# A graph layer on one Trainium2 core: x enters the gate products in three f32r products, x plus beta moves within its turn, and setup and passage are re-ordered

## The reference

```python
h = concat([x[src], x[dst]])
msgs = silu(h @ W1.T + b1) @ W2.T + b2
agg = segment_sum(msgs, src) / (count(src) + 1e-08)
gi, gh = agg @ w_ih.T + b_ih, x @ w_hh.T + b_hh
r, z = sigmoid(i_r + h_r), sigmoid(i_z + h_z)
n = tanh(i_n + r * h_n)
x_new = (1 - z) * n + z * x
y = layernorm(x + gamma * layernorm(x_new) + beta)
```

## Time and profile before

| | |
|---|---|
| median of 3 runs | 2478.14 us (2478.11 to 2478.32) |
| profiled execution, its time | 2478.47 us |
| its span | 2476.8 us, mean granted clock of TensorE 0.987 |
| busy | PE 2301.0, PEld 1622.0, DVE 2122.0, ACT 1496.2, POOL 1332.4 us |
| DMA | 520.31 MB, mean 210 GB/s |

### The profile page before, as it was taken

One profiled execution on the slowest core, in us unless ns is written; L12 is line 12 of the kernel. 1 busy time (PEld: TensorE's weight loads), 2 busy tenths in 40 slices (PEclk: granted clock), 3 DMA queues, 4 the chain that ended last, 5 costly groups with the idle time before them and its releaser, 6 DMA issues.

```text
span 2476.8 us, 46628 instructions
## 1 busy us (share of the span) xinstructions
PE 2301.0 (93%) x10234; PEld 1622.0 (65%) x10234; DVE 2122.0 (86%) x6136; ACT 1496.2 (60%) x2955; POOL 1332.4 (54%) x1475
## 2 busy tenths in 40 slices
PE   4999999999999995999999999999999999999995
PEld 2888888888888883655555555555555555555553
DVE  4777777777777764899999999999999999999998
ACT  2444444444444442577767777777677777777776
POOL 3444444444444421566666666666666666666663
PEclk9999999999999997999999999999999999999998
DMA  3566666666666655666666666666666666666662
GB/s 105 213 232 227 229 230 228 230 227 231 225 233 225 234 209 193 200 216 216 213 210 213 214 217 205 216 207 210 203 212 213 210 205 212 215 209 212 209 204 94
DMA packets 192600, 520.31 MB, mean 210 GB/s; under 512 B 51362, under 2 KB 53946, under 8 KB 192572
## 3 DMA queue, kind: packets, MB, share of 16 engines
q1 hardware_dynamic: 117308, 313.53, 36.2%
q0 software_dynamic: 75264, 206.47, 25.5%
HBM read 468.02 MB, written 206.73 MB: 272 GB/s over the span
## 4 chain that ended last, share of the span: by engine, by line
DVE 42%; PE 37%; issue 15%; DVEq 3%; DMA 1%; ACT 1%; SPq 0%; POOL 0%; POOLq 0%; ACTq 0%
PE banks L893 34%; DVE zd L824 6%; DVE xn L830 5%; DVE st L871 5%; DVE diff L819 5%; DVE rhn L807 5%; DVE tg L835 4%; DVE uu L846 4%; PE banks L905 4%; DVE oh L798 3%; DVE ag L877 2%; DVE ve L860 1%; DVEq L798 1%; DVEq L191 1%; DVE nm L855 1%
## 5 line engine op out<-in xcount | busy, mean ns | idle before, releaser
L893 PE MATMUL banks<-whh,xts 128*128 128x512 f32 (+1 forms) x3136 | 1089.9, 485 | 0.0
L893 PEld LDWEIGHTS banks<-whh,xts 128*128 128x128 f32 x3136 | 552.4, 190 | 312.5 <-issue 281.7
L346 POOL DMA_INDIRECT mg<-messages,rows_now x392 | 408.1, 1041 | 170.4 <-POOL rows_now L383 87.1
L404 POOL TENSOR_TENSOR xb<-xs,betab 128x512 f32<-128x512 f32 x196 | 249.0, 1270 | 372.5 <-ACT rz L501 372.5
L346 POOL DMA_INDIRECT xsrc<-in_x,src_now x196 | 187.3, 956 | 438.5 <-PE banks L905 433.0
L893 PE MATMUL banks<-mg,oh 128*128 128x512 f32 (+1 forms) x1568 | 322.1, 348 | 108.7 <-issue 57.2
L893 PEld LDWEIGHTS banks<-mg,oh 128*128 128x128 f32 x1568 | 253.2, 189 | 214.9 <-issue 158.7
L525 ACT ACTIVATE yy<-uu,nmr,rs 128x256 f32<-128x256 f32 x392 | 214.0, 593 | 293.0 <-DVE nmr L866 293.0
L513 ACT ACTIVATE banks<-banks,rcount 128x768 f32<-128x768 f32 x392 | 326.7, 871 | 38.0 <-PE banks L893 24.9
L471 ACT ACTIVATE msg<-banks 128x512 fp32r<-128x512 f32 (+1 forms) x392 | 192.8, 492 | 246.7 <-PE banks L893 218.3
L625 DVE TENSOR_TENSOR msg<-banks,msg 128x512 fp32r<-128x512 f32 (+1 forms) x392 | 199.9, 552 | 160.1 <-issue 137.7
(11 more groups left out here) (129 smaller groups left out, 4248.8 us busy)
## 6 DMA issues: line engine op xcount, KB each, us to landing
messages<-msg SPq DMA_DIRECT2D x196, 772.0 KB
xts<-in_xt SPq DMA_DIRECT2D x196, 256.0 KB
xs<-in_x SPq DMA_DIRECT2D x196, 256.0 KB
out_y<-yy SPq DMA_DIRECT2D x196, 256.0 KB, 5.1
mg<-messages,rows_now POOLq DMA_INDIRECT x392
xsrc<-in_x,src_now POOLq DMA_INDIRECT x196
xdst<-in_x,dst_now POOLq DMA_INDIRECT x196
oh<-counts SPq DMA_DIRECT2D x196, 2.0 KB
```

Of the source, the lines that this page charges most:

```text
L346: nc.gpsimd.indirect_dma_start(out=dst_tile, out_offset=None, in_=rows, in_offset=bass.IndirectOffsetOnAxis(ap=table, axis=0), bounds_chec ...
L404: nc.gpsimd.tensor_tensor(out=xb[:, u, :], in0=xs[:, u, :], in1=betab[:, :], op=ALU.add)\
L893: return nc.tensor.matmul(out_, lhsT, rhs, start=start, stop=stop, skip_group_check=skip)
```

## The change

x enters the gate products as its f32r high part times both parts of `whh` plus its low part times the high one. `xh` is made by ScalarE at the end of its turn, `xl` by GpSimd behind `tg`. `add_beta` moves to the end of GpSimd's turn and waits for `ag` (aggregate1) instead of the gates. The one hots move behind `st` with lag 2. The transposed load is issued one turn earlier. In the setup the order of the weight loads changes, the row vectors of the biases are loaded as broadcasts, their TensorE products go, and the chain of bias steps runs beside the first edge slots. In the passage the table, the counts, the fill of `mg` (now ScalarE and GpSimd) and the count stores run beside the last edge slots, and a sigmoid over one column is run ahead of the node stage. Some tiles change their place in memory.

```diff
-        whh = sb("whh", [P, KC, G3])
+        wxh, wxl = sb("wxh", [P, KC, G3], f32r), sb("wxl", [P, KC, G3], f32r)
...
+        xh, xl = sb("xh", [P, QU, 2 * D], f32r), sb("xl", [P, QU, 2 * D], f32r)
...
-        def edge_slots(eng, part, first=0):
+        def edge_slots(eng, part, first=0, also=None):
             for n in range(first, EDGE_HEAD):
                 part(n // 8, n % 8)
+                if also is not None:
+                    also(n)
...
+        def store_counts(eng, c):
+            b0, b1 = CHUNKS[c]
+            eng.dma_start(counts[:, b0 * P:b1 * P].rearrange("r (b l) -> b r l", l=P),
+                          count_rows[0:b1 - b0, c, :, :]).then_inc(cn_put, 16)
...
-            more = [(wih[:, :, :], wiht.rearrange("(k p) n -> p k n", p=P)),
-                    (w2s[:, :, :], w2.rearrange("(k p) n -> p k n", p=P)),
-                    (brow[:, 0:3 * D], bih.rearrange(row, a=1)),
-                    (brow[:, 3 * D:6 * D], bhh.rearrange(row, a=1)),
+            more = [(b2s[:, k:k + 1], b2[k * P:(k + 1) * P].rearrange("(p a) -> p a", a=1)) for k in range(KC)]
+            more += [(b1s[:, k:k + 1], b1[k * P:(k + 1) * P].rearrange("(p a) -> p a", a=1)) for k in range(KC)]
+            more += [(w2s[:, :, :], w2.rearrange("(k p) n -> p k n", p=P)),
+                    (wih[:, :, :], wiht.rearrange("(k p) n -> p k n", p=P)),
                     (whh[:, :, :], whht.rearrange("(k p) n -> p k n", p=P)),
+                    (bias_gate[:, :], bih.rearrange(row, a=1).to_broadcast([P, G3])),
+                    (total[:, 0, :], bhh.rearrange(row, a=1).to_broadcast([P, G3])),
...
-            sp.wait_ge(cn_cp, 2)
-            store_counts()
...
-                need(sp, S["n_mm"], q - QU + 1)
+                need(sp, S["n_xl"], q - QU + 1)
...
-            node_turns(sp, ((load_counts, 3), (load_x, 3), (load_rows, 2), (store_y, -7)), first=-3, last=7)
+            node_turns(sp, ((load_counts, 3), (load_x, 4), (load_rows, 2), (store_y, -7)), first=-4, last=7)
...
+            pool.wait_ge(rb_ready, 2)
+            for m in range(KC):
+                pool.wait_ge(e_hid[m], TILES // QUAD)
+                pool.wait_ge(e_sl[m], TILES // QUAD)
+            for u in range(QU // 2, QU):
+                for h in range(2):
+                    nc.gpsimd.tensor_copy(mg[:, u, h, :], bias_rows[:, :].bitcast(f32)).then_inc(mg_zero, 1)
+            pool.wait_ge(tab_ready, 1)
+            pool.wait_ge(mg_zero, 2 * QU)
             for u in range(EU):
                 pool.wait_ge(e_stored[u], 16 * (TILES // EU))
-            pool.wait_ge(tab_ready, 1)
-            pool.wait_ge(mg_zero, 2 * QU)
...
+                def x_lo(q, u):
+
+                    if not isinstance(q, int) or q >= 5:
+                        pool.wait_ge(S["n_tg"], q - 4)
+                    pool.wait_ge(S["n_xh"], q + 1)
+                    need(pool, S["n_mm"], q - QU + 1)
+                    nc.gpsimd.tensor_tensor(out=xl[:, u, :], in0=xts[:, u, :], in1=xh[:, u, :].bitcast(f32),
+                                            op=ALU.subtract).then_inc(S["n_xl"], 1)
+
                 def add_beta(q, u):
 
-                    pool.wait_ge(S["n_rz1"], min(q + 2, PAIRS) if isinstance(q, int) else q + 2)
+                    pool.wait_ge(S["n_a1"], min(q + 2, PAIRS) if isinstance(q, int) else q + 2)
...
-                node_turns(pool, ((add_beta, -2), (gather_rows, 4), (inv_std1, -2), (inv_std2, -5)), first=-4, last=5)
+                node_turns(pool, ((gather_rows, 4), (inv_std2, -5), (x_lo, 2), (inv_std1, -2), (add_beta, -2)), first=-4, last=5)
...
+            nc.scalar.activation(wxh[:, :, :], whh[:, :, :], ACT.Copy).then_inc(wx_hi, 1)
+            act.wait_ge(wx_lo, 1)
             act.wait_ge(rb_mm, 1)
             nc.scalar.activation(bias_c[:, 0:2 * D], p_hid[:, 0, :], ACT.Copy).then_inc(rb_cp, 1)
             nc.scalar.activation(bias_c[:, 2 * D:G3], p_hid[:, 1, 0:D], ACT.Copy).then_inc(rb_cp, 1)
-            nc.scalar.activation(bias_gate[:, 0:2 * D], p_g[:, 0, :], ACT.Copy).then_inc(rb_cp, 1)
-            nc.scalar.activation(bias_gate[:, 2 * D:G3], p_g[:, 1, 0:D], ACT.Copy).then_inc(rb_cp, 1)
-            nc.scalar.activation(b_hi[:, :], p_g[:, 1, D:2 * D], ACT.Copy).then_inc(rb_cp, 1)
-            act.wait_ge(rb_ready, 1)
-            edge_slots(act, edge_slot, first=QUAD)
+
+            def tail(n):
+                if n == TILES + 4:
+                    act.wait_ge(rb_ready, 2)
+                    for m in range(KC):
+                        act.wait_ge(e_hid[m], TILES // QUAD)
+                        act.wait_ge(e_sl[m], TILES // QUAD)
+                if n >= TILES + 4:
+                    k = n - TILES - 4
+                    nc.scalar.activation(mg[:, k // 2, k % 2, :], bias_rows[:, :].bitcast(f32), ACT.Copy).then_inc(mg_zero, 1)
+                if n == TILES + 5:
+                    for r, bank in enumerate((p_cnt, p_tab)):
+                        act.wait_ge(cn_mm, r + 1)
+                        by_chunk = bank.rearrange("p (c l) -> p c l", l=P)
+                        nc.scalar.activation(count_rows[:, 0:3, r, :], by_chunk[:, 0:3, :], ACT.Copy).then_inc(cn_cp, 1)
+                        nc.scalar.activation(count_rows[0:BLOCKS - 3 * P, 3, r, :], by_chunk[0:BLOCKS - 3 * P, 3, :], ACT.Copy)\
+                            .then_inc(cn_cp, 1)
+                if n == TILES + 6:
+                    act.wait_ge(cn_cp, 4)
+                    for c in range(len(CHUNKS)):
+                        store_counts(act, c)
...
+            edge_slots(act, edge_slot, first=QUAD, also=tail)
+            act.wait_ge(ld_c, 16)
+            nc.scalar.activation(warm[:, :], ident[:, 0:1], ACT.Sigmoid)
+
+            def x_hi(q, u):
+                act.wait_ge(got_xt[u], 16 * (nth(q, u) + 1))
+                need(act, S["n_mm"], q - QU + 1)
+                nc.scalar.activation(xh[:, u, :], xts[:, u, :], ACT.Copy).then_inc(S["n_xh"], 1)
...
-            node_turns(act, ((last_norm, -6), (tanh, -1), (gates0, 0), (mean_scale, 1), (squares, -4), (gates1, 0)), first=-1, last=7)
+            node_turns(act, ((last_norm, -6), (tanh, -1), (gates0, 0), (mean_scale, 1), (squares, -4), (gates1, 0), (x_hi, 3)), first=-3, last=7)
...
-            dve.wait_ge(ld_w, 16 * W_LOADS)
-            for k in range(KC):
-                nc.vector.tensor_scalar(b2b[:, k, :], ones[:, :].bitcast(f32), b2s[:, k:k + 1], None, ALU.mult)\
-                    .then_inc(b2_ready, 1)
...
+            dve.wait_ge(wx_hi, 1)
+            nc.vector.tensor_tensor(wxl[:, :, :], whh[:, :, :], wxh[:, :, :].bitcast(f32), ALU.subtract).then_inc(wx_lo, 1)
...
+            def bias_step(n):
+                if n == QUAD:
+                    nc.vector.memset(bias_rows[:, :].bitcast(f32), 0.0).then_inc(rb_step, 1)
+                    nc.vector.tensor_copy(b_hi, hn_all).then_inc(rb_step, 1)
+                if n == QUAD + 1:
+                    dve.wait_ge(rb_mm, 1)
+                    nc.vector.memset(msg[:, :, LOC:HALF].bitcast(f32), 0.0).then_inc(node_const, 1)
+                    nc.vector.memset(msg[:, :, HALF + G3:ROW].bitcast(f32), 0.0).then_inc(node_const, 1)
+                    nc.vector.tensor_tensor(bias_gate[:, 0:2 * D], bias_gate[:, 0:2 * D], total[:, 0, 0:2 * D], ALU.add)\
+                        .then_inc(rb_step, 1)
+                    dve.wait_ge(rb_step, 2)
+                    nc.vector.tensor_tensor(b_lo, hn_all, b_hi.bitcast(f32), ALU.subtract).then_inc(rb_step, 1)
...
+            def tail(n):
+                bias_step(n)
+                if n == TILES + 1:
+                    dve.wait_ge(e_one, 3 * TILES)
+                    nc.vector.reduce_max(top[:, :], ranks[:, :], axis=mybir.AxisListType.X).then_inc(lv_top, 1)
+                    dve.wait_ge(e_tab, TILES)
+                    nc.vector.tensor_copy(edges_of[:, :], p_cnt[:, 0:BLOCKS]).then_inc(cn_ready, 1)
+                    nc.vector.tensor_scalar(at_least_1[:, :], p_cnt[:, 0:BLOCKS], 1.0, None, ALU.max).then_inc(cn_ready, 1)
+                if n == TILES + 2:
+                    table_fields(t_step)
+                if n == TILES + 3:
+                    table_rows(t_step, 0, tab_ready)
...
-            node_turns(dve, ((gated_h, -1), (n_input, -1), (var_eps2, -5), (residual, -4), (one_hot, 3), (minus_mean, -4),
-                             (subtract_n, -1), (z_diff, -1), (x_new, -1), (scale_gamma, -3), (stats1, -1), (shift, -5),
-                             (aggregate1, -1), (var_eps1, -1)), first=-3, last=5)
+            node_turns(dve, ((gated_h, -1), (n_input, -1), (var_eps2, -5), (residual, -4), (minus_mean, -4),
+                             (subtract_n, -1), (z_diff, -1), (x_new, -1), (scale_gamma, -3), (stats1, -1), (one_hot, 2), (shift, -5),
+                             (aggregate1, -1), (var_eps1, -1)), first=-2, last=5)
...
-            mm(p_g[:, 0, :], one, brow[:, 0:2 * D], True, False)
-            mm(p_g[:, 0, :], one, brow[:, 3 * D:5 * D], False, True)
```

(22 more changed lines are left out.)

159 lines of the change are left out of this document (77 added, 82 removed).

## The result

The changed kernel takes 2542.8 us (median of 4 runs, 2534.5 to 2550.9) against 2478.1 before: a ratio of 1.0261 (95% interval 1.0246 to 1.0276). The forecast was 2542, with slower as the likelier side. The profiled execution took 2543.84 us, its span is 2542.2.

The account below looks back on a forecast made before the run. VectorE bounds the node stage before; afterwards the landing of y's store was to bind, a turn of 7.95 us against 7.50. Sum: 2478.5 + 88 (turns) − 10 (setup) − 14 (passage) = 2542 us, range 2420 to 2615.

Parts of the forecast that it names:

- The mechanism that decides: Node stage: store of y issued a turn later behind x+beta; squares, gates and rhn wait; turn 7.95 us, +88 us.
- L: Node stage: time from issue to landing of a store of y, taken as 4.5 us, bounded by 3.1 and 7.2.
- 2T = 11.4 + L: Node stage: loop over two turns through ag, x+beta, store, squares and gates; 15.9 us, so a turn T of 7.95.
- rival 1: Node stage: the store lands in time (L up to 3.4), VectorE sets the turn at 7.4; 2434 us, chance 0.18.
- rival 4: Node stage: the store lands as now, L = 5.2 or more, turn 8.3 us; 2611 us, chance 0.16.
- VectorE's turn, 7.4: Node stage: VectorE's own turn, 6.72 us plus 0.60 for one hots held by x_lo, within 6.7 and 7.7.
- Rival 3: Node stage: store in time, x_lo late each second turn, holding one hots 1.1 us; turn 7.65, 2484 us, chance 0.14.
- nmr, −0.78: Node stage, VectorE: moving x+beta away frees the small product nmr, 0.916 to 0.14 us, 0.78 us a turn.
- One-hot lag 2: nothing: Node stage: one hots at lag 2 instead of 3 change nothing, as the tanh is still covered by other VectorE rows.
- TensorE 1.3 us lighter a turn, 250 us in all: Node stage: 24 f32r products (4.2 us) replace fp32 ones (5.56 us) each turn; by itself worth nothing.
- Setup −10: Setup: TensorE waits less before the first edge slot, 38.2 against 48.9; −10 us net, within −7 and −11.
- Passage −14: Between edge and node stage: work moves beside the last edge slots, start at 961; −14 us, within −10 and −16.

Follow-up runs that it names:

- e1: Changed kernel with the sync queue storing y ahead of the row load: 2506.5 us, 1.0118 of the kernel before.
- e2: Changed kernel with the squares writing their scratch to a tile of their own, sync queue order untouched: 2507.4 us, 1.0120 of the kernel before.
- e8: Changed kernel, store of y ahead of the row load, GpSimd's subtraction for x's low part left out (output differs, for measuring only): 2343.9 us.
- e4: Kernel before with only x+beta moved late and the store of y put ahead of the row load: 2508.0 us, 1.0119 of the kernel before.
- e5: As e4, plus the one hots with lag 2 behind the statistics: 2377.9 us, 0.9595 of the kernel before.
- e11: Changed kernel, store of y ahead of the row load, x's low part made by VectorE instead of GpSimd: 2447.6 us, 0.9883 of the kernel before.
- e6: Changed kernel, store of y ahead of the row load, x entering by plain f32 products without the split: 2338.4 us, 0.9438 of the kernel before.
- e12: As e6, with GpSimd's four fills of the message buffers started behind VectorE's last message part: 2334.6 us, 0.9428 of the kernel before.
- e9: Changed kernel's setup and passage with the whole node part of the kernel before: 2447.3 us, 0.9878 of the kernel before.

## Why the prediction was right, and where it was not

- **The mechanism that decides**: right in kind. The squares wait for the store (206 us in all), the gates and `rhn` behind them, and e1 and e2 both take 36 us back by removing that wait in two ways. The store's issue, forecast 2.2 us into VectorE's turn, is there (2.16 in the median). But the loop does not bind in each turn, as the forecast had it. It binds in 37 of 195, mostly behind one buffer's stores.
- **That the number is met is luck.** The turn of 7.95 was measured as 7.912, +83 us for +88, and setup with passage gave 19 for 24. I took L = 4.5 for every store. Most take 2.9 to 3.0 us; by 2T = 11.4 + L that is a turn of 7.2, below VectorE's own, so it doesn't bind (the condition of rival 1 holds there). One in four takes 5.0, near the L of rival 4. And VectorE's own turn without the store is 7.73 and not 7.4. So 7.912 is 7.73 with a late `rhn` now and then, and not half of 15.9. Where it binds, the sum is near: from the turns of 8.07 and 9.45 us that begin at 1440.71 the landing takes 5.6 (issue to squares), which leaves 11.9 for my 11.4, of which 0.5 is `ag` ending at 7.8 and not 7.3.
- **The median of the earlier trace rows**, 5.2, on which L rests: in the profile before, the view places the landings of 40 of these 160 stores only, all of one buffer, and I read it as that of all.
- **VectorE's turn, 7.4**: mis-sized. The base of 6.72 was too low: with no hold by x_lo the turn is 6.907, since `nm` is still held (291 ns in e8) and some 0.2 us of short waits stay. And x_lo costs 0.82 and not 0.60 a turn. Where it starts on time the one hots lose 0.54, near the 0.60; where GpSimd's queue makes it late they lose 0.69 or 1.27, and `ve` loses 0.12. Rival 3 had this in kind (7.65, late in each second turn by 1.1); with the store in time its 2484 was measured as 2506. The Trainium skill (SBUF — State Buffer, Who interferes with whom) states the exclusive lock by which, as the prediction worked it out, one hots had to lose 0.72 rather than 0.60. Where `xl` starts on time they lose 0.54 by the rows, so the direction holds and the whole length is not met; that the mean is 0.72 too comes from the late starts.
- **nmr, −0.78**: right, 0.916 to 0.170.
- **"One-hot lag 2: nothing"**: a wrong reading that did the number no harm, since the change contains the new place. As a part of the change it decides whether moving x+beta can pay at all (e4 to e5, 130 us). I looked for what waits on VectorE for the one hots and not for what the one hots wait: gathers that GpSimd issues behind the moved x+beta.
- **TensorE 1.3 us lighter a turn, 250 us in all**: 123 us (2301.0 to 2178.4). At the full clock its turn is 324.65 / 400 × 7.446 = 6.04 (e11) against 7.02 before, 0.98 lighter; the rest went to the clock, below. That it is worth nothing held: e8, with the lighter products, takes 5.6 us more than e6.
- **Setup −10**: −10.9 (first edge slot at 37.97, forecast 38.2).
- **Passage −14**: −8.0. The setup brings everything 10.9 us forward, but the last message comes only 953.94 − 946.49 = 7.5 earlier, and from there to the first copy of rows it takes 9.9 and not the 961 − 953.94 = 7.1 of the forecast. I gave GpSimd's fills no price because I looked at who was idle, not at what they hold on VectorE; on e6, e12 shows that they delay the last message by 6.4 us and the first `rhn` by 3.9. Of the 9.9 us, 3.9 (against e9's 6.0) go with GpSimd's `x_lo` and stay open.
- **Rival 1, the store in time**: its landing was there for three buffers of four, but not its turn of 7.4; with every store in time (e1) the kernel still takes 2506. The other side of no change is reached only when the low part leaves GpSimd as well (e11, 2448) or x goes in undivided (e6, 2338).
